# Cross-attention in a perceiver block: the row maxima taken off by VectorE, the sums of the probabilities moved to GpSimd

## The reference

```python
q1 = split_heads(x1 @ Wq1, N1)                 # 8 heads of 64
k = concatenate([split_heads(x1 @ Wk1, N1), split_heads(x2 @ Wk2, N2)], axis=1)
v = concatenate([split_heads(x1 @ Wv1, N1), split_heads(x2 @ Wv2, N2)], axis=1)
sim = einsum('bihd,bjhd->bhij', q1, k) * d ** -0.5
attn = softmax(sim, axis=-1)                   # over 256 + 4096 keys
out = einsum('bhij,bjhd->bihd', attn, v).reshape(B, N1, h * d)
return out @ Wo + bo
```

## Time and profile before

| | |
|---|---|
| median of three executions | 1659.54 us |
| profiled execution, its time | 1661.31 us |
| its span, first to last instruction | 1659.3 us |
| mean granted TensorE clock | 0.961 |
| cross-attention | until about 1160 us of the span |

### The profile page before, as it was taken

The page is one execution under the profiler, slowest core; times in us unless marked ns, Lnnn a source line. Parts: engine busy times, 40 slices in busy tenths (PEclk is TensorE's granted clock), DMA queues, the critical chain, the costliest instruction groups (busy, mean ns, idle before and its releaser), DMA issues. The chain is left out here.

```text
span 1659.3 us, 29603 instructions
## 1 busy us (share of the span) xinstructions
PE 1489.4 (90%) x11988; PEld 1121.4 (68%) x11988; DVE 1124.6 (68%) x1283; ACT 712.1 (43%) x971; POOL 443.8 (27%) x286
## 2 busy tenths in 40 slices
PE   4999999999999999999999999998597777827995
PEld 4877777776777777777777777766354444527995
DVE  2687578657657765865876685685676999644663
ACT  3443345443444543444454444333345333224773
POOL 4300003200000320100131000000133999433885
PEclk8999999999999999999999999999797999958998
DMA  5000021000002100000300000000304900092333
GB/s 174 14 11 11 1 84 51 1 14 11 11 15 87 36 2 14 20 1 27 99 11 2 23 11 2 2 1 1 84 10 178 231 0 0 1 362 63 63 59 58
DMA packets 62388, 76.50 MB, mean 46 GB/s; under 512 B 6385, under 2 KB 47985, under 8 KB 61857
## 3 DMA queue, kind: packets, MB, share of 16 engines
q1 hardware_dynamic: 57168, 68.51, 13.6%
q0 software_dynamic: 5088, 6.11, 2.5%
HBM read 58.39 MB, written 17.25 MB: 46 GB/s over the span
## 5 line engine op out<-in xcount | busy, mean ns | idle before, releaser
L537 DVE TENSOR_REDUCE xa_maxes<-psum 128x2 f32<-128x1024 f32 (+1 forms) x288 | 334.2, 1162 | 265.0 <-PE psum L741 264.9
L467 ACT ACTIVATE xa_probs<-psum 128x1024 f32<-128x1024 f32 x272 | 268.7, 1026 | 273.2 <-PE psum L774 272.8
L558 DVE TENSOR_TENSOR xa_prob_sum<-xa_prob_sum,xa_probs 128x1024 f32<-128x1024 f32 x240 | 313.1, 1305 | 11.3 <-ACT xa_probs L467 10.5
L786 PE MATMUL psum<-xa_probs,xa_vals 128*64 128x256 f32 x2176 | 280.5, 389 | 2.0 <-DVE xa_heads_T L572 1.5
L786 PEld LDWEIGHTS psum<-xa_probs,xa_vals 128*64 128x64 f32 x2176 | 139.4, 136 | 104.6 <-issue 41.8
L458 ACT ACTIVATE xa_vals<-psum 128x512 f32<-128x512 f32 x136 | 81.2, 597 | 207.6 <-PE psum L666 207.6
L768 PE MATMUL psum<-xa_q_hi,xa_k_hi 64*128 64x256 f32 x1088 | 156.4, 283 | 0.6 <-issue 0.6
L666 PE MATMUL psum<-xa_wv_hi,xa_ctx_hi 128*128 128x256 f32 x512 | 150.7, 294 | 4.4 <-DVE xa_maxes L537 4.4
L772 PE MATMUL psum<-xa_q_hi,xa_k_lo 64*128 64x256 f32 x1088 | 154.3, 279 | 0.0
L774 PE MATMUL psum<-xa_neg_max,xa_ones 64*128 64x256 f32 x1088 | 154.2, 279 | 0.0
L770 PE MATMUL psum<-xa_q_lo,xa_k_hi 64*128 64x256 f32 x1088 | 153.8, 278 | 0.0
(11 more groups left out here) (329 smaller groups left out, 3019.5 us busy)
## 6 DMA issues: line engine op xcount, KB each, us to landing
xa_ctx_in<-in_ctxT_dram SPq DMA_DIRECT2D x32, 512.0 KB, 3.8
ex_slots<-mx_blank_tile SPq DMA_DIRECT2D x2, 4372.5 KB, 37.5
xa_stage<-in_L_xattn_Wk_dram SPq DMA_DIRECT2D x32, 128.0 KB, 2.4
xa_stage<-in_L_xattn_Wv_dram SPq DMA_DIRECT2D x16, 256.0 KB, 3.1
ex_raw<-in_L_ffn_w_gate_dram SPq DMA_DIRECT2D x8, 512.0 KB, 10.1
ex_raw<-in_L_ffn_w_up_dram SPq DMA_DIRECT2D x8, 512.0 KB, 10.8
ex_raw<-in_L_ffn_w_down_dram SPq DMA_DIRECT2D x8, 512.0 KB, 11.6
ex_xt<-ex_slots SPq DMA_DIRECT2D x15, 265.0 KB, 2.8
```

Source lines behind the costliest of these rows:

```text
L467: nc.scalar.activation(probs[:, n % RING, :], S[:, 2 * (n % 2):2 * (n % 2) + 2, :].rearrange("p h q -> p (h q)"), ACT.Exp, scale=HD ** -0. ...
L537: dve.tensor_reduce(maxes[:, qt, :, g:g + 1], max_banks(v, g, qt)[:, :, 0:group_keys(g)[1]], AX_X, ALU.max).then_inc(max_reduced, 1)
L558: dve.tensor_tensor(prob_sum[:, :], prob_sum[:, :], probs[:, n % RING, :], ALU.add).then_inc(summed, 1)
L786: i = pe.matmul(O[half[h], 0:N1], vals[:, 2 * j + t, lanes:lanes + HD], probs[:, n % RING, (2 * h + t) * N1:(2 * h + t + 1) * N1], start=( ...
```

## The change

- `score` loses the product with ones. VectorE's new `shift` subtracts the maxima (`max_rows`, kept for both heads on all partitions) from the scores in PSUM and writes to the ring `probs`; the exponential works in place there. `score` of tile n now waits until `shift` of tile n-2 is done, `shift` waits for the scores, and for the ring (`weigh` and `add_probs` of tile n-4), `exponentials` waits for `shift`.
- `turn_maxima` has four products instead of two, with the maximum broadcast as the stationary operand; `store_max` copies 512 elements out of PSUM instead of negating 256.
- `add_probs` moves from VectorE to GpSimd, two a step from step 1 on, ahead of GpSimd's other work of the step; `fold_sums` adds the two key halves in the last step, and `sum_probs` has two products instead of four, and waits for the fold.
- On TensorE, `project_queries(u + 2)` moves ahead of the last `weigh` and of the value tiles of the last step. VectorE's queue in a step becomes: reduce, shift(2d), reduce, shift(2d+1), split of keys. ScalarE's order is as it was.

```diff
+            def add_probs(u, j):
+                n = u * HG + j
+                pool.wait_ge(exp_done, n + 1)
+                if j == 1:
+                    if u > 0:
+                        pool.wait_ge(sums_ready, u)
+                    pool.tensor_tensor(prob_sum[:, :], probs[:, (n - 1) % RING, :], probs[:, n % RING, :],
+                                       ALU.add).then_inc(summed, 1)
+                else:
+                    pool.wait_ge(summed, sums_done(n) - 1)
+                    pool.tensor_tensor(prob_sum[:, :], prob_sum[:, :], probs[:, n % RING, :],
+                                       ALU.add).then_inc(summed, 1)
+
+            def fold_sums(u):
+
+                both = prob_sum[:, :].rearrange("p (h t q) -> p h t q", h=2, t=2)
+                pool.wait_ge(summed, (u + 1) * (HG - 1))
+                pool.tensor_tensor(both[:, :, 0, :], both[:, :, 0, :], both[:, :, 1, :], ALU.add).then_inc(folded, 1)
...
             for u, d in steps():
+                if d >= 1:
+                    add_probs(u, 2 * d - 1)
+                    add_probs(u, 2 * d)
+                if d == STEPS - 1:
+                    fold_sums(u)
...
             def exponentials(u, j):
                 n = u * HG + j
-                if n >= RING:
-                    act.wait_ge(pv_done, n - RING + 1)
-                    act.wait_ge(summed, sums_done(n - RING))
-                act.wait_ge(scores_ready, n + 1)
-                nc.scalar.activation(probs[:, n % RING, :], S[:, 2 * (n % 2):2 * (n % 2) + 2, :].rearrange(
-                    "p h q -> p (h q)"), ACT.Exp, scale=HD ** -0.5).then_inc(exp_done, 1)
+                act.wait_ge(shifted, n + 1)
+                nc.scalar.activation(probs[:, n % RING, :], probs[:, n % RING, :], ACT.Exp,
+                                     scale=HD ** -0.5).then_inc(exp_done, 1)
...
             def reduce_rows(v):
                 dve.wait_ge(max_reduced, (v + 1) * NG * QT)
-                dve.tensor_reduce(max_cols[:, :, 0:P:HD], maxes[:, :, :, :], AX_X, ALU.max).then_inc(rowmax_done, 1)
-
-            def store_neg_max(v):
+                dve.tensor_reduce(row_max[:, :, :], maxes[:, :, :, :], AX_X, ALU.max).then_inc(rowmax_done, 1)
+
+            def store_max(v):
                 dve.wait_ge(max_turned, v + 1)
-                dve.tensor_scalar(neg_max[:, :], M[:, 1, 0:N1], -1.0, None, ALU.mult).then_inc(neg_max_ready, 1)
-
-            def add_probs(u, j):
+                if v > 0:
+                    dve.wait_ge(shifted, v * HG)
+                dve.tensor_copy(max_rows[:, :, :].rearrange("p h q -> p (h q)"), M[:, 1, :]).then_inc(max_ready, 1)
+
+            def shift(u, j):
+
                 n = u * HG + j
-                dve.wait_ge(exp_done, n + 1)
-                if j == 1:
-                    if u > 0:
-                        dve.wait_ge(sums_ready, u)
-                    dve.tensor_tensor(prob_sum[:, :], probs[:, (n - 1) % RING, :], probs[:, n % RING, :],
-                                      ALU.add).then_inc(summed, 1)
-                else:
-                    dve.wait_ge(summed, sums_done(n) - 1)
-                    dve.tensor_tensor(prob_sum[:, :], prob_sum[:, :], probs[:, n % RING, :],
-                                      ALU.add).then_inc(summed, 1)
+                dve.wait_ge(scores_ready, n + 1)
+                if j == 0:
+                    dve.wait_ge(max_ready, u + 1)
+                if n >= RING:
+                    dve.wait_ge(pv_done, n - RING + 1)
+                    dve.wait_ge(summed, sums_done(n - RING))
+                dve.tensor_tensor(probs[:, n % RING, :].rearrange("p (h t q) -> p h t q", h=2, t=2),
+                                  S[:, 2 * (n % 2):2 * (n % 2) + 2, :].rearrange("p h (t q) -> p h t q", t=2),
+                                  max_rows[:, :, :].unsqueeze(2).broadcast_to([P, 2, 2, N1]),
+                                  ALU.subtract).then_inc(shifted, 1)
...
                 v = u + 1
@@ -604,40 +629,33 @@
                         split_keys(v, 0)
                         if own_due(u, d) is not None:
                             split_own(own_due(u, d))
-                    if u > 0:
-                        add_probs(u - 1, HG - 1)
+                    shift(u, 0)
                     if v < U:
                         reduce_max(v, 0, 0)
+                    shift(u, 1)
+                    if v < U:
                         split_keys(v, 1)
-                    add_probs(u, 1)
                     continue
                 if v < U:
                     reduce_max(v, d - 1, 1)
                 if d == 1 and u > 0:
                     invert_sums(u - 1)
                     normalize(u - 1)
-                if d >= 2 and not (d == STEPS - 1 and v < U):
-                    add_probs(u, 2 * d - 1)
+                shift(u, 2 * d)
                 if v < U:
                     reduce_max(v, d, 0)
                 if d == 2 and u > 0 and u % PAIRS == 0:
                     add_output(u // PAIRS - 1)
                 if d < STEPS - 1:
-                    add_probs(u, 2 * d)
+                    shift(u, 2 * d + 1)
                     if v < U:
                         split_keys(v, d + 1)
                 elif v < U:
                     reduce_max(v, d, 1)
                     reduce_rows(v)
-
-                    if u % 2 == 1:
-                        add_probs(u, 2 * d - 1)
-                    store_neg_max(v)
+                    store_max(v)
                     if u + 2 < U:
                         split_q(u + 2)
-                    if u % 2 == 0:
-                        add_probs(u, 2 * d - 1)
-            add_probs(U - 1, HG - 1)
...
                 if v > 0 and (g, qt) == (NG - 1, 1):
 
-                    pe.wait_ge(exp_done, v * HG - 1)
+                    pe.wait_ge(shifted, v * HG - 1)
...
-                for qt in range(QT):
-                    i = pe.matmul(M[:, 1, qt * P:(qt + 1) * P], max_cols[:, qt, :], ident[:, :],
-                                  start=True, stop=True)
+                for h in range(2):
+                    for qt in range(QT):
+                        i = pe.matmul(M[:, 1, h * N1 + qt * P:h * N1 + (qt + 1) * P],
+                                      row_max[:, qt, h:h + 1].broadcast_to([P, P]), ident[:, :],
+                                      start=True, stop=True)
                 i.then_inc(max_turned, 1)
 
             def score(u, j):
                 n, g = u * HG + j, (j + 1) // 2
                 if n >= 2:
-                    pe.wait_ge(exp_done, n - 1)
-                if j == 0:
-                    pe.wait_ge(neg_max_ready, u + 1)
+                    pe.wait_ge(shifted, n - 1)
                 pe.wait_ge(k_split, u * NG + g + 1)
                 q = [(x[half[h], u % 2, :]) for x in (q_hi, q_lo) for h in range(2)]
                 for t in range(2):
@@ -769,9 +787,7 @@
                     for h in range(2):
                         pe.matmul(out[h], k[h], q[2 + h], start=False, stop=False)
                     for h in range(2):
-                        pe.matmul(out[h], k[2 + h], q[h], start=False, stop=False)
-                    for h in range(2):
-                        i = pe.matmul(out[h], ones[half[h], :], neg_max[half[h], :], start=False, stop=True)
+                        i = pe.matmul(out[h], k[2 + h], q[h], start=False, stop=True)
                 i.then_inc(scores_ready, 1)
...
             def sum_probs(u):
-                pe.wait_ge(summed, (u + 1) * (HG - 1))
-                for t in range(2):
-                    for h in range(2):
-                        i = pe.matmul(O[half[h], N1:2 * N1], ones[:, 0:HD].bitcast(F32),
-                                      prob_sum[:, (2 * h + t) * N1:(2 * h + t + 1) * N1],
-                                      start=(t == 0), stop=(t == 1))
+                pe.wait_ge(folded, u + 1)
+                for h in range(2):
+                    i = pe.matmul(O[half[h], N1:2 * N1], ones[:, 0:HD].bitcast(F32),
+                                  prob_sum[:, 2 * h * N1:(2 * h + 1) * N1], start=True, stop=True)
                 i.then_inc(sums_ready, 1)
 
             def project_output(b):
...
                     weigh(u, weighed[1])
                     score_for_max(v, d, 1, values)
+                    if u + 2 < U:
+                        project_queries(u + 2)
                     weigh(u, HG - 1)
                     for c, j in v_due(u, d):
                         project_values(c, j, maxima)
                         values += 1
-                    if u + 2 < U:
-                        project_queries(u + 2)
                     turn_maxima(v, values)
```

More of the change, by code:

```diff
@@ L228, in cross_attention @@
         max_turned = sem("xa_max_turned")
-        neg_max_ready = sem("xa_neg_max_ready")
+        max_ready = sem("xa_max_ready")
+        shifted = sem("xa_shifted")
         scores_ready = sem("xa_scores_ready")
@@ L233, in cross_attention @@
         pv_done = sem("xa_pv_done")
```

(5 more changed lines are left out.)

7 lines of the change are left out of this document (3 added, 4 removed).

## The result

| | before | after |
|---|---|---|
| median (4 runs each, same chip) | 1659.90 us (1658.64 to 1662.66) | 1738.36 us (1733.94 to 1743.31) |
| ratio, 95% interval | | 1.047 [1.044, 1.050] |
| profiled execution, its span | 1661.31, 1659.3 us | 1743.31, 1741.6 us |
| mean granted TensorE clock | 0.961 | 0.950 |
| largest wait of VectorE on one line | 264.9 us, reduces, for TensorE | 213.8 us, splits of keys, for ScalarE |

The change makes the kernel 4.7% slower. The forecast was 1728 us with a range of 1700 to 1757: the side, the cause and the range held, the middle lay 10 us low.

The account below looks back on a forecast made before the run. TensorE was taken to set the 6.03 us plain step, VectorE 0.8 us behind. Terms 36.9 - 15.0 + 21 + 6.4 - 1 + 0 + 7.3 + 13.1 = +68.7 us gave 1728 us, range 1700 to 1757.

Parts of the forecast that it names:

- the price of a pair: TensorE, plain steps: two score products side by side take 0.118 us; four pairs fewer save 0.47 us a step.
- the value steps: Odd units' steps with two value tiles: the loop hides there; 23 x -0.29 and 12 contended x -0.69, together -15.0 us.
- the plain step: Step with no values projected: 6.03 us before, set by TensorE; 6.85 us afterwards, 45 steps, +36.9 us.
- the loop: Plain steps: split of keys waits for ScalarE's store, behind an exponential awaiting VectorE's second subtraction; 6.85 us, 0.82 more; chance 0.82.
- TensorE stays the bound: Rival: VectorE's chain stays under 6.03 us or the store gets out early, removed pairs count in full; about 1606 us; chance 0.05.
- each sign named for it: Plain steps: 6.8 to 6.9 us, VectorE idle 1.6 us before each split, released by ScalarE; TensorE idle 1.3 us.
- Contention: Rival: GpSimd's additions stretch VectorE's subtraction to 2.5 us, +1.3 or more in 60 steps, some 1810 us; chance 0.05.
- The ring of four lets that run late: GpSimd's two additions, 4.8 us a step, 7.2 with a chunk, may run late and catch up within 6.85 or 9 us steps.
- The last step of a unit: Last score saves 0.24 us, moved queries' projection adds 0.7 us in odd units: 7 x 0.47 against 8 x -0.4, sum 0.
- Odd units' steps 0 and 1: Step 0 from 7.69 to 7.8 us, step 1 from 5.65 to 8.4 us: 7 x 3.0, +21 us.
- Clock: TensorE's clock drops after waits in 3 of 7 odd units, +9.6 us, and once at the end, +3.5: +13 us.
- The last unit: GpSimd sets the end with additions of 2.4 us each: 34.1 us becomes 40.5, +7.3 us; clock at the end +3.5.

Follow-up runs that it names:

- experiment 6: Kernel before the change with only the four products with ones of each tile left out: 1627.6 us, ratio 0.981.
- experiment 1: Changed kernel with ScalarE's store of the next group's keys moved between the two exponentials of a step: 1660.9 us, ratio 1.001.
- experiment 2: Extra 448-element ScalarE copy before each split of keys is released: changed kernel 1768.3 us; with the store between the exponentials 1665.8 us.
- experiment 5: Changed kernel with the queries' projection put back behind the value tiles, ahead of the turn: 1731.6 us, ratio 1.043.
- experiment 8: Changed kernel with store between exponentials, weights' subtraction ahead of GpSimd's second last-step addition, six last-unit tiles added by VectorE: 1638.2 us, ratio 0.987.
- experiment 10: Kernel of experiment 8 with VectorE inverting the sums and normalizing at the end of step 0 instead of in step 1: 1638.0 us, ratio 0.988.
- experiment 4: Changed kernel with GpSimd's subtraction for the next key weights moved ahead of its second addition of the last step: 1729.4 us, ratio 1.041.
- experiment 3: Changed kernel with GpSimd adding only the first two tiles of each unit, the other 15 additions left out: 1713.3 us, ratio 1.032.
- experiment 9: Kernel of experiment 8 with the first product of the keys' projection issued ahead of the coarse scores on TensorE: 1658.4 us, ratio 0.998.

## Why the prediction was right, and where it was off

- **What bounds the kernel before.** TensorE, as said, and the price of a pair was 0.118 us; but leaving four of them out of a step gives 0.26 us, not 0.47 (experiment 6). The prediction had half the reason in hand, the wait of `score_for_max(d,0)` for a reduce at 0.18 us, and booked it for the value steps only, where it held (8.98 measured, 8.95 forecast). In the plain step it left it out. The forecast of the time didn't suffer, since the loop's 6.83 lay over 5.56 and 5.77 alike. The figure for the rival "TensorE stays the bound" did: with the loop open the kernel takes 1661 us, not 1606, and 31 of the 55 are this (64 us against experiment 6's 33).
- **The loop.** 6.85 forecast, 6.83 measured, and each sign named for it was there: 1.61 us ahead of the split for ScalarE, and a wait of TensorE, at 1.00 and not 1.3, since its own work takes 5.77 us and not 5.56. Experiments 1 and 2 show it from both sides. The exponential from SBUF took 1.059 against 1.026 us, 0.03 more; the estimate from the 52 cycles of the Trainium skill's VectorE: DVE Perf Modes (errata of TRN2) was 0.04, and the trace agrees.
- **Contention.** No subtraction took over 1.23 us, the chunks no longer cost (value steps in unit 3 at 8.98 where the earlier trace rows has 9.64). Right.
- **GpSimd's queue.** Here a step failed, and it is 9 of the 13 us that are missing. "The ring of four lets that run late" was true of the exponentials, but not of the 0.7 us subtraction of the weights, which the additions were put ahead of and for which TensorE begins to wait 3.6 us after the turn's first product: 9 us in units 3, 7 and 11. The prediction named who waits for the fold, and not who waits for what is queued behind it.
- **The last step of a unit.** Forecast +0.47 in odd and -0.4 in even units, measured +0.68 and -0.44. The queries' projection on the path of odd units costs 0.9 us and not 0.7 (experiment 5). In sum +1.2 us instead of 0.
- **Odd units' steps 0 and 1.** 3.0 each forecast, 3.1 measured, units 3, 7 and 11 with the queue's cost on top. The terms written down for step 0 add to 7.69 us and not to the 7.8 given, and 3.0 was rounded up; it took 445.52 - 437.53 = 7.99 in unit 5.
- **Clock.** 9.6 us forecast, 8.9 measured, by luck: six drops of seven at 1.5 us each, not three at 3.2. The 3.2 came from a drop with 6.4 us at half clock; in step 2 TensorE ran at the half (1.2 GHz) for some 3.4 us only (1.7 us lost, from the shares of full clock, of which 1.5 reached the step). Timeline and stretches of unit 5:

```profile
455.25 0.50 PE L759 MATMUL psum<-xa_k_hi,xa_q_hi 64*128 64x512 f32 x2 [2.50 <-issue]
```

```profile
452.00:456.00 4.00, 1.50 (x15) 1.08 (x14) 2.67 (x3) 1.29 (x2) 3.35 (x2) 0.97 0.00 0
456.00:460.00 4.00, 4.00 (x15) 2.31 (x15) 2.54 (x3) 2.48 (x4) 2.41 (x2) 0.61 0.00 0
```

- **The last unit.** 10.8 forecast with its clock, 13.2 measured. An in-place addition started every 2.50 us (37.57 for 15), not every 2.4: 1.5 us of the difference. The output projection at half clock was foreseen, 6.72 against 3.72 us.
- **Even units' first steps.** +6.4 forecast, +5.9 measured from the turn's first product: the turn takes 0.5 us more, step 0 behind it gives 0.6 to 0.9 back (1.8 in unit 0), and step 1 takes 1.15 more.

The sum was 13 us low against its own profiled execution: 9.0 for the unforeseen queue, 2.4 for the last unit, 1.3 for the value steps, 1.2 for the last steps; the other terms came within 1 us each. The range had room for it, though its upper end isn't what its terms give: 7.1 us steps, all drops and dear additions add up to some 1762 us, not 1757.

## What to carry to other kernels

When an operation is put between two others on a second engine, write out what stands behind its follower in the third engine's queue, and ask whether the first engine waits for that: a loop through two in-order queues costs its whole length in every step, however idle both engines are. It may be cut by moving one store: here that made up for the whole loss, and two more edits in the other queues (experiment 8) turned the change into a gain of 1.3%. An operation of 0.7 us that is queued behind 6 us of other work is as late as all of it; go through each queue for who waits for what comes last.

## What the runs showed of the hardware that was not expected

- A wait of the same length may or may not drop TensorE's clock: 1.85 us kept it in unit 5 and lost it in unit 9 of one execution (experiment 10); 2.50 us lost it in unit 5 of the changed kernel, and kept it in unit 5 of experiment 4's (granted clock 1.00 through the step). A drop lengthened such a step by 1.4 to 2.9 us (experiments 3, 4, 5 and 10). A forecast can only count such places.
- When VectorE and GpSimd both add from SBUF, the one that begins second takes longer by about what the other has left: VectorE 3.18 instead of 1.22 us, GpSimd 3.43 instead of 2.39; the first keeps its time (experiment 8). A subtraction with one operand in PSUM is not touched (1.23 us at most).
- On TensorE a change between half-row pairs and full-row products costs 0.1 to 0.2 us (experiment 9), as much as one to two pairs of score products; which part of the change costs it is open.
